# Expert tiles and the second layer's rotation in one stage, the q and k products made once

## What is computed

```
qkv = (x @ qkv_w.T).reshape(Bb, Ss, 3, H, D)
...
q = _rope(q, c, s)          # [t1*c - t2*s, t1*s + t2*c], t1 and t2 the halves of a head
k = _rope(k, c, s)
scores = jnp.einsum('bhqd,bhkd->bhqk', q, k) * SCALE
attn = jax.nn.softmax(scores + kb[None], axis=-1)
...
idx = jnp.argmax(router_probs, axis=-1)
h = jax.nn.relu(jnp.einsum('te,td,edf->tf', onehot, xn, W1) + b1[idx])
y = (jnp.einsum('te,tf,efd->td', onehot, h, W2) + b2[idx]) * gates
```

## Time and profile before

| | us |
|---|---|
| median of 3 runs (lowest, highest) | 3034.65 (3034.45, 3037.06) |
| the profiled execution | 3035.2 |
| its span in the trace | 3033.5 |
| TensorE busy | 2781.9 (92%) |
| VectorE busy | 2486.9 (82%) |
| GpSimd busy | 2499.3 (82%) |
| ScalarE busy | 1558.0 (51%) |

### The profile page before, as it was taken

The page is one execution under the profiler, slowest core; times in us unless marked ns, Lnnn a source line. Parts: engine busy times, 40 slices in busy tenths (PEclk is TensorE's granted clock), DMA queues, the critical chain, the costliest instruction groups (busy, mean ns, idle before and its releaser), DMA issues. The chain is left out here.

```text
span 3033.5 us, 46671 instructions
## 1 busy us (share of the span) xinstructions
PE 2781.9 (92%) x17656; PEld 1156.8 (38%) x17656; DVE 2486.9 (82%) x3379; ACT 1558.0 (51%) x1889; POOL 2499.3 (82%) x1205
## 2 busy tenths in 40 slices
PE   5959999999999999997399689999999999999997
PEld 3413333333333333332374233333333333333333
DVE  6568888888888888884438799999999999999995
ACT  4325555555555555553122245555555555555554
POOL 0009999999999999996237669999999999999997
PEclk8979999999999999998599889999999999999998
DMA  4250111111111111100312421121211111112100
GB/s 110 87 194 20 33 32 30 29 29 29 29 29 29 29 29 29 29 1 1 92 35 102 174 56 55 56 56 56 56 56 56 56 56 56 56 56 56 55 1 14
DMA packets 63824, 155.27 MB, mean 51 GB/s; under 512 B 18017, under 2 KB 33770, under 8 KB 61426
## 3 DMA queue, kind: packets, MB, share of 16 engines
q1 hardware_dynamic: 62578, 150.20, 17.7%
q0 software_dynamic: 1024, 2.10, 0.2%
HBM read 113.34 MB, written 38.93 MB: 50 GB/s over the span
## 5 line engine op out<-in xcount | busy, mean ns | idle before, releaser
L938 POOL TENSOR_TENSOR a_sums<-a_sums,room 128x1024 f32<-128x1024 f32 x512 | 1196.2, 2363 | 65.8 <-ACT room L788 42.4
L699 PE MATMUL a_ov<-room,va 128*64 128x512 f32 x4096 | 994.0, 606 | 0.0
L777 ACT ACTIVATE room<-room,sscale 128x1024 f32<-128x1024 f32 x512 | 588.6, 1150 | 505.3 <-DVE room L873 505.3
L840 DVE TENSOR_REDUCE a_mx<-a_jb 128x1 f32<-128x1024 f32 x501 | 611.5, 1221 | 129.1 <-PE a_jb L653 122.7
L938 POOL TENSOR_TENSOR a_sums<-room 128x1024 f32<-128x1024 f32 x256 | 603.7, 2359 | 95.2 <-ACT room L781 49.0
L835 DVE CUSTOM_DVE_ANT_0 a_junk<-a_jb,a_tab 128x1024 bf16<-128x1024 f32 x501 | 609.6, 1217 | 62.8 <-DVE a_m L846 36.9
L873 DVE TENSOR_TENSOR room<-a_st,a_tab 128x1024 f32<-128x1024 f32 x512 | 624.1, 1220 | 14.2 <-PE a_st L688 12.9
L788 ACT ACTIVATE room<-a_st,sscale 128x1024 f32<-128x1024 f32 x256 | 285.3, 1114 | 358.9 <-PE a_st L688 358.9
L652 PE MATMUL a_jb<-a_kh,a_qh 64*128 64x512 f16 x1002 | 386.9, 386 | 41.4 <-DVE a_mx L840 25.7
L688 PE MATMUL a_st<-a_qh,a_kh 64*128 64x512 f16 x2048 | 391.0, 378 | 0.0
L688 PE MATMUL a_st<-a_ql,a_kh 64*128 64x512 f16 x2048 | 389.9, 377 | 0.0
(11 more groups left out here) (219 smaller groups left out, 2590.7 us busy)
## 6 DMA issues: line engine op xcount, KB each, us to landing
a_tab<-bias_line SPq DMA_DIRECT2D x16, 1984.0 KB, 10.7
qk_high<-q_oh SPq DMA_DIRECT2D x32, 512.0 KB, 2.6
qk_low<-q_ol SPq DMA_DIRECT2D x32, 512.0 KB, 3.6
a_qh<-qk_high SPq DMA_DIRECT2D x64, 256.0 KB, 4.4
a_kh<-qk_high SPq DMA_DIRECT2D x64, 256.0 KB, 5.0
a_ql<-qk_low SPq DMA_DIRECT2D x64, 256.0 KB, 7.4
a_kl<-qk_low SPq DMA_DIRECT2D x64, 256.0 KB, 7.7
ex_w<-in_L_ffn_W SPq DMA_DIRECT2D x1, 2048.0 KB, 10.4
```

What stands on the lines that cost most here:

```text
L699: last = nc.tensor.matmul(ov[t * DH:(t + 1) * DH, :], k.va[:, 2 * s + t, h * DH:(h + 1) * DH], prob[:, step % RING, t * QC:(t + 1) * QC], ...
L777: nc.scalar.activation(prob[:, r, :], prob[:, r, :], ACT.Exp, scale=k.sscale[:, layer:layer + 1])\
L840: nc.vector.reduce_max(mx[:, j // 2, j % 2:j % 2 + 1], scratch(n, j), AX.X).then_inc(max_done, 1)
L938: nc.gpsimd.tensor_tensor(a, first, prob[:, step % RING, :], ALU.add).then_inc(summed, 1)
```

## The change

`middle_stages` takes the place of the expert stages and of `qkv_stage` for layer 1. In `route_stage` TensorE and ScalarE now make 8 of the 16 tiles of values (three of them before the ranking), the expert biases are loaded there, and GpSimd sorts the q and k weights so that all first halves of the heads stand together, and all second halves (`grouped`, in `k.wo`). In `experts_and_rotation_stage` there are 16 jobs of 256 rows by 1024 tokens. TensorE makes the product of the first halves (`low_part`) and of the second halves (`high_part`) once each; VectorE makes the four products with cosine and sine from them and, after each pair of two, a low half of the job before; GpSimd makes the difference and the sum, each begun when a low half is done; ScalarE makes the high halves. Jobs 1 to 12 carry the 23 expert tiles, two a job: ScalarE picks weights, rectifies all four quarters and copies tiles in and out, which GpSimd and VectorE did in part. Jobs 12 to 15 carry the other 8 tiles of values, two each. `tp`, `dn`, `low_part` and `high_part` are single. The gathers and the 16 Silu move into `attention_stage`.

```diff
+            if bias:
+                act.wait_ge(gathered, 16 * NT)
+                for q in range(NT):
+                    nc.scalar.activation(k.gate[:, q, :], k.gate[:, q, :], ACT.Silu, scale=k.prob[:, q:q + 1])
...
+            if bias:
+                for q in range(NT):
+                    nc.gpsimd.indirect_dma_start(k.gate[:, q, :], None, k.sorted_out[:, :],
+                                                 bass.IndirectOffsetOnAxis(ap=k.spot[:, q:q + 1], axis=0))\
+                      .then_inc(gathered, 16)
...
+            halves = k.w1[:, 0:2, :].rearrange("p i (h r d) -> p i h r d", h=H, r=2)
+            grouped = flat(k.wo[:, :, :]).rearrange("p (i r h d) -> p i r h d", i=2, r=2, h=H)
+            for i in range(2):
+                for r in range(2):
+                    nc.gpsimd.tensor_copy(grouped[:, i, r, :, :], halves[:, i, :, r, :])
...
+            def values_of(q):
+                if q >= 2:
+                    pe.wait_ge(val_copied, q - 1)
+                for c in range(2):
+                    last = nc.tensor.matmul(val[:, q % 2, c * QC:(c + 1) * QC], k.xnT[:, q * P:(q + 1) * P],
+                                            k.w1[:, 2, c * QC:(c + 1) * QC], start=True, stop=True)
+                last.then_inc(valued, 1)
+
+            for q in range(3):
+                values_of(q)
             pe.wait_ge(counted, 6)
             pe.wait_ge(added, 1)
             nc.tensor.matmul(tot[:, :], k.ones[:, :], before[:, 0, 2 * NT - 1, :], start=True, stop=True)
             nc.tensor.matmul(flat(pos[:, :, :]), tri[:, :], flat(onehot[:, :, :]), start=True, stop=False)
             nc.tensor.matmul(flat(pos[:, :, :]), k.ones[:, :], flat(before[:, 0, NT - 1:2 * NT - 1, :]),
                              start=False, stop=True).then_inc(ranked, 1)
+            for q in range(3, NVAL):
+                values_of(q)
 
...
+            for q in range(NVAL):
+                act.wait_ge(valued, q + 1)
+                nc.scalar.activation(k.va[:, q, :], val[:, q % 2, :], ACT.Copy).then_inc(val_copied, 1)
+                if q == 3:
+                    act.wait_ge(shifted, 1)
+                    nc.scalar.activation(e[:, :, :], e[:, :, :], ACT.Exp).then_inc(exped, 1)
...
+        low_part, high_part = m.ps("er_low_part", [P, 1024]), m.ps("er_high_part", [P, 1024])
+        up = m.ps("er_up", [P, 2, FT, P])
+        dn = m.ps("er_dn", [P, 4, D])
+        tp = m.ps("er_tp", [P, 4, P])
...
+        jobs = [(g, i, half) for g in range(4) for i in range(2) for half in range(2)]
+        NJOB = len(jobs)
+        work = [[i for i in range(TL) if 1 + i // 2 == j] for j in range(NJOB)]
+        late = [[q for q in range(NVAL, NT) if NJOB - (NT - q + 1) // 2 == j] for j in range(NJOB)]
...
+            def project(j):
+                g, i, half = jobs[j]
+                for r, (part, ready) in enumerate(((low_part, a_ready), (high_part, b_ready))):
+                    if j >= 1:
+                        pe.wait_ge(prod, 4 * (j - 1) + 3 + r)
+                    for c in range(2):
+                        q0 = half * 1024 + c * 512
+                        last = nc.tensor.matmul(part[:, c * 512:(c + 1) * 512], wqk[:, i, r, g * P:(g + 1) * P],
+                                                k.xnT[:, q0:q0 + 512], start=True, stop=True)
+                    last.then_inc(ready, 1)
...
+                if i % 4 == 0 and i >= 4:
+                    pe.wait_ge(y_copied, i // 4)
...
+            def values_of(q):
+                m = q - NVAL
+                if m == 0:
+                    pe.wait_ge(relu_done, TL)
+                for c in range(2):
+                    if m >= 1:
+                        pe.wait_ge(val_copied, 2 * (m - 1) + c + 1)
+                    nc.tensor.matmul(flat(up[:, c, :, :]), k.xnT[:, q * P:(q + 1) * P], k.w1[:, 2, c * QC:(c + 1) * QC],
+                                     start=True, stop=True).then_inc(valued, 1)
+
...
+            project(0)
+            owners = [pe.value_load(tiles[0:1, i:i + 1], min_val=0, max_val=NE - 1) for i in range(TL)]
...
+            for j in range(NJOB):
+                if j >= 1:
+                    project(j)
+                for i in work[j]:
+                    if i == 0:
+                        pe.wait_ge(b1_copied, 1)
+                        turn(0)
+                    if i % 4 == 0 and i // 4 + 1 < NG:
+                        turn(i // 4 + 1)
+                    upward(i)
+                    if i >= 1:
+                        downward(i - 1)
+                    if i == TL - 1:
+                        downward(i)
+                for q in late[j]:
+                    values_of(q)
...
+            def high_half(j, r):
+                if j >= 2:
+                    act.wait_ge(high_stored[j % 2], 32 * (j // 2))
+                act.wait_ge(rot, 2 * j + r + 1)
+                nc.scalar.activation(split[:, j % 2, 0, r, :], (first, second)[r][:, j % 2, :], ACT.Copy)\
+                  .then_inc(high, 1)
...
+                for f in range(FT):
+                    last = nc.scalar.activation(hT[:, i % 2, f, :], up[:, i % 2, f, :], ACT.Relu,
+                                                bias=b1t[:, f, i:i + 1])
+                last.then_inc(relu_done, 1)
+                if i + 2 < TL:
+                    pick(i + 2)
+                if i % 4 == 0 and i >= 4:
+                    copy_y(i // 4 - 1)
+                if i == TL - 1:
+                    copy_y(NG - 1)
...
+            for j in range(NJOB):
+                if j >= 1:
+                    high_half(j - 1, 0)
+                for i in work[j][:1]:
+                    tile(i)
+                if j >= 1:
+                    high_half(j - 1, 1)
+                for i in work[j][1:]:
+                    tile(i)
+                for q in late[j]:
+                    copy_values(q)
+            for r in range(2):
+                high_half(NJOB - 1, r)
...
+            def low_half(j, r):
+                rotated = (first, second)[r]
+                ve.wait_ge(high, 2 * j + r + 1)
+                if j >= 2:
+                    ve.wait_ge(low_stored[j % 2], 32 * (j // 2))
+                nc.vector.tensor_tensor(split[:, j % 2, 1, r, :], rotated[:, j % 2, :], split[:, j % 2, 0, r, :],
+                                        ALU.subtract).then_inc(low, 1)
+
+            for j, (g, i, half) in enumerate(jobs):
+                b, sl = j % 2, slice(half * 1024, (half + 1) * 1024)
+                ve.wait_ge(a_ready, j + 1)
+                if j >= 2:
+                    ve.wait_ge(low, 2 * j - 2)
+                nc.vector.tensor_tensor(first[:, b, :], low_part[:, :], cos[:, sl], ALU.mult).then_inc(prod, 1)
+                ve.wait_ge(b_ready, j + 1)
+                if j >= 1:
+                    ve.wait_ge(rot, 2 * j - 1)
+                nc.vector.tensor_tensor(product[:, 0, :], high_part[:, :], sin[:, sl], ALU.mult).then_inc(prod, 1)
+                if j >= 1:
+                    low_half(j - 1, 0)
+                nc.vector.tensor_tensor(second[:, b, :], low_part[:, :], sin[:, sl], ALU.mult).then_inc(prod, 1)
+                if j >= 1:
+                    ve.wait_ge(rot, 2 * j)
+                nc.vector.tensor_tensor(product[:, 1, :], high_part[:, :], cos[:, sl], ALU.mult).then_inc(prod, 1)
+                if j >= 1:
+                    low_half(j - 1, 1)
+            for r in range(2):
+                low_half(NJOB - 1, r)
+
+        @block.gpsimd
+        def _(pool):
+            for j in range(NJOB):
+                b = j % 2
+                pool.wait_ge(prod, 4 * j + 2)
+                if j >= 1:
+                    pool.wait_ge(low, 2 * j - 1)
+                nc.gpsimd.tensor_tensor(first[:, b, :], first[:, b, :], product[:, 0, :], ALU.subtract).then_inc(rot, 1)
+                pool.wait_ge(prod, 4 * j + 4)
+                if j >= 1:
+                    pool.wait_ge(low, 2 * j)
+                nc.gpsimd.tensor_tensor(second[:, b, :], second[:, b, :], product[:, 1, :], ALU.add).then_inc(rot, 1)
+            nc.gpsimd.tensor_copy(flat(k.wo[:, :, :]), flat(k.wo1[:, :, :]))
```

More of the change, by code:

```diff
@@ L1164, in expert_tiles_stage @@
[L1164 to L1167, removed]
+        b1t = m.sb("er_b1t", [P, FT, TL])
+        first, second, product = (m.sb("er_first", [P, 2, 1024]), m.sb("er_second", [P, 2, 1024]),
+                                  m.sb("er_product", [P, 2, 1024]))
@@ L1174, in _, with xsT @@
+        def xsT(a, b):
+            return xsT_first[:, a:b, :] if b <= NT else xsT_more[:, a - NT:b - NT, :]
         @block.sync
         def _(sp):
[L1176 to L1184, removed]
@@ new lines, in rows_of, with store_high @@
+            def rows_of(store, j):
+                g, i, half = jobs[j]
+                rows = store[i].rearrange("a p s -> (a p) s").rearrange("(g h r d) s -> g r h d s", g=4, h=4, r=2)
+                return [rows[g, r, :, :, half * 1024:(half + 1) * 1024] for r in range(2)]
+            def store_high(j):
```

(39 more changed lines are left out.)

153 lines of the change are left out of this document (85 added, 68 removed).

## The result

| | us |
|---|---|
| before, median of 4 runs (lowest, highest) | 3034.69 (3034.45, 3037.06) |
| after, median of 4 runs (lowest, highest) | 2997.38 (2997.3, 2998.8) |
| ratio, 95% interval | 0.9869 (0.9856 to 0.9881) |
| the profiled execution after, its span | 2997.3, 2995.6 |

The change gains 37.3 us where the forecast had 75.6. The time lies above the whole range, which ended at 2982. The direction held, and so did the parts before and behind the joined stage; the missing 38 us are all within it. The stretch of 239.1 us became 198.1, which is 41.0 less. The joined stage starts 1.6 us later than the expert stage did (1489.26 for 1487.62), and from attention's first issue to the end pass 1.4 us more (1308.2 for 1306.8), so the span falls by 37.9.

What follows compares the result with a forecast made beforehand. It took TensorE to bound the expert tiles and VectorE the rotation, one after the other, 239.1 us; joined, TensorE-bound tile jobs make 159.7. 79.4 less, minus 2.3 route and 1.5 gathers, saves 75.6: 3034.65 to 2959, range 2944 to 2982.

Steps and rivals of the forecast that it cites:

- Part 1, route: Route stage: three value tiles ahead of the ranking delay the scatters by 2.3 us, bounds +0.5 to +6.1.
- Part 2, start: Joined stage's start: 15.4 us to project(1), or 20.5 if the 23 owner reads wait for project(0).
- Rival C: Joined stage's start: the owner reads wait for project(0), alone; 2964 us, inside the forecast's range, no chance of its own.
- Part 3, jobs: Joined stage: job 1 10.7 us, jobs 2 to 11 86.9, then 11.35, 7.25, 8.2, and 19.9 to the end.
- the five waits for the y copy: Jobs 2 to 11: five waits of about 0.3 us each, since the y copy's PSUM tile is now single.
- the case in which the tail would be 0.9 shorter: Joined stage's tail: the last low half but one meets a sum that began first and waits; tail 0.9 us shorter.
- Tile jobs are bound by TensorE: Jobs 2 to 11: TensorE needs 8.35 us a job and VectorE less, so TensorE, not VectorE, sets the period.
- Part 4, gathers: Attention's start: 16 gathers and Silu moved there, 1 MB more ahead of the first maxima; +1.5 us (0 to 5).
- A (waits hidden): Tile jobs: TensorE's waits hide behind long passes, a job takes 7.3 us; kernel 2946, chance 0.12.
- B: Tile jobs: ScalarE's order couples in, second low half waits behind tile i; about 10.5 us a job, 2982, chance 0.20.
- D, the engines taking turns: Tile jobs: TensorE and VectorE alternate, 15.9 us a job if fully closed; 3046, decides from 13.7, chance 0.02.
- the range's lower bound: Whole kernel: 2944 us, from -9 for half of A's waits, -1.8 route and -1.5 gathers.

Runs made afterwards that it cites:

- the store mended: The changed kernel with q and k weight columns sorted (d, h), so a store's destination has 32 outermost in place of 4: 2957.57 us, ratio 0.9747.

## Why the prediction was wrong

- **Part 1, route:** forecast +2.3 us. The value passes took 6.96 us (forecast 6.9), the first scatter came 1.3 later, or 1.7 with the 0.4 by which that execution was ahead at the logits (1448.05 for 1448.43). That is 0.6 under the forecast and within its bounds.
- **Part 2, start:** 15.5 us to project(1), forecast 15.4. The reads run beside project(0). Rival C falls.
- **Part 3, jobs: the step that failed.** The terms add up TensorE's and VectorE's work; nowhere is there one for the stores. SyncE's issues were left as they had been, 32 of 512 KB, with a tail of "about 5" from the last low half. Doubling their number and halving them was not weighed, nor the destination's new form, which `rows_of` in the changed kernel's code gives. From project(1) to project(15) pass 142.9 us for 124.4, 18.5 more; from there to the end 39.7 for 19.9, 19.8 more. With 0.1 at the start that is the 38.4 by which 198.1 exceeds 159.7. Half of it is the tail: the last stores stand behind others, and nothing is left to hide them.
- **The same terms with the store mended** hold: job 1 10.9 (10.7), jobs 2 to 11 83.9 (86.9), job 12 11.3 (11.35), 13 7.2 (7.25), 14 8.4 (8.2), job 15 to the end 18.9 (19.9). The sum is 156.1 for 159.7, the kernel 2957.6 for 2959. Of the 3 us in jobs 2 to 11, 2.5 are the five waits for the y copy (1.5) and the 0.1 a job for semaphores, neither of which came: TensorE was never idle there. Another 0.4 is a slip: 3.43 + 2 x 2.39 + 0.1 is 8.31 and not 8.35. In the tail the low half began 0.05 us before the sum (1633.09 and 1633.14), so it kept its 1.22 and the sum took 3.38; the case in which the tail would be 0.9 shorter by the Trainium skill's rule did not arise. The tail is 1.0 shorter since only 2.95 us pass from the last low half's end, 1639.42, to the stage's end, where 4.6 were taken from stores of twice the size; the last low half itself took 1.73 in place of 1.22, beside a copy of GpSimd's that had begun before it. "Tile jobs are bound by TensorE" was right of the work and wrong of the kernel, in which the stores were the bound.
- **Part 4, gathers:** first exponent 0.6 later, forecast 1.5, and 1.4 more from attention's first issue to the end. Right within its bounds.
- **Rivals:** A (waits hidden) didn't come, even with the store mended: 8.39 a job and not 7.3. B gave 10.5 a job, near the 10.7 found, but by ScalarE waiting for TensorE; it waited for DMAs, 46.2 us in all, so the nearness is luck. D, the engines taking turns, didn't come: no tile job reached its 13.7. The terms given for the range's lower bound (-9, -1.8, -1.5) add up to 2947 and not 2944, which changes nothing here.

Rows ahead of the prediction held the price of an engine: the old rotation moved 128 GB/s at a share of 0.32, which is 5.1 engines, so 25 GB/s an engine. No row held the number of engines; only the 4 in `rows_of` did, for a reader who asks what it does to a store. A job stores 1.05 MB: over four engines 10.5 us, more than the 8.4 of work, in 15 jobs some 30 us, and more for the tail.

## What to carry to other kernels

When a change rewrites where a DMA goes, read the access pattern's outermost dimension on both sides, divide GB/s by share times 16 for the rate of one engine, and put the transfer as an engine of its own into the sum of a pipeline's period. A DMA share that stays flat at a simple fraction such as 0.25, with issues that take microseconds instead of half of one, is the sign of it. Often the cure is an order of dimensions, with the data sorted earlier to suit: here it gained 40 us with a few changed lines.

## What the runs showed of the hardware that I had not expected

- A store of 256 KB from 128 partitions ran at 51 or 102 GB/s by the outermost dimension of its DRAM destination alone (2, 4), and with 32 the stretch moved the 139 GB/s that the jobs asked for. Stores issued from a second queue shared the same four engines, and the kernel got 35 us slower.
- Once the engines are behind, SyncE's issue itself grows from 0.5 to 2.45 us, and to 5.0 with two engines. A y store queued behind such stores landed after 11.7 us in place of 2.3.
- 23 register reads at a stage's start left TensorE idle for 13.34 us before, and for 7.80 after, beside project(0). Spread over the jobs they cost TensorE nothing that the trace shows, and the stage got some 5 us shorter.
